# A GNN layer on one core: the last edge chunk moved with 128 partitions, chunk 0's messages earlier, two powers joined

## The reference, cut to what matters

```python
h = jnp.maximum(_layernorm(x), 0.0)
xn = layernorm(h, g1, b1)
msg = relu(xn[src] + edge_attr)
aggr = segment_sum(msg, dst, num_segments=N)
t = (1.0 + eps_gin) * xn + aggr
t = relu(t @ Wg1 + bg1) @ Wg2 + bg2
y = h + t
f = gelu(layernorm(y, g2, b2) @ Wf1 + bf1) @ Wf2 + bf2
out = x + y + f
```

## Time and profile before

| | |
|---|---|
| runs | 1043.13, 1045.61, 1047.68 us |
| median | 1045.61 us |
| profiled execution, its own time | 1042.96 us |
| its span (first to last instruction) | 1041.2 us |
| mean granted TensorE clock | 0.985 of full speed |
| PE busy | 982.8 us, 94% |
| DVE busy | 965.1 us, 93% |
| ACT busy | 852.8 us, 82% |
| POOL busy | 825.9 us, 79% |

### The profile page before, as it was taken

One profiled execution on the slowest core, in us unless ns is written; L12 is line 12 of the kernel. 1 busy time (PEld: TensorE's weight loads), 2 busy tenths in 40 slices (PEclk: granted clock), 3 DMA queues, 4 the chain that ended last, 5 costly groups with the idle time before them and its releaser, 6 DMA issues. The chain is left out here.

```text
span 1041.2 us, 23085 instructions
## 1 busy us (share of the span) xinstructions
PE 982.8 (94%) x6684; PEld 857.0 (82%) x6684; DVE 965.1 (93%) x3499; ACT 852.8 (82%) x2158; POOL 825.9 (79%) x510
## 2 busy tenths in 40 slices
PE   1569999999999999999999999999999999999978
PEld 0357888988889889889888889889889889888867
DVE  5979999999999999999999999999999999998642
ACT  1458888898888988988888988988988988978853
POOL 7788888888788888888888888888888888876610
PEclk9869999999999999999999999999999999999999
DMA  7856766877886654555654664654654554543221
GB/s 259 228 165 162 204 172 179 242 230 220 253 238 157 160 130 118 157 133 117 156 135 116 154 139 116 157 136 115 158 134 116 150 140 117 125 105 81 51 60 41
DMA packets 110468, 156.87 MB, mean 151 GB/s; under 512 B 24835, under 2 KB 50607, under 8 KB 110334
## 3 DMA queue, kind: packets, MB, share of 16 engines
q1 hardware_dynamic: 70358, 128.99, 39.0%
q0 software_dynamic: 37760, 25.66, 17.7%
q10 hardware_dynamic: 2216, 0.66, 0.3%
HBM read 90.61 MB, written 64.61 MB: 149 GB/s over the span
## 5 line engine op out<-in xcount | busy, mean ns | idle before, releaser
L451 POOL DMA_INDIRECT aggr_sums<-e_merged,e_index x196 | 339.2, 1731 | 80.6 <-issue 70.7
L939 PE MATMUL p_out<-wf,n_act 128*128 128x128 f32 x3136 | 370.5, 276 | 1.6
L939 PEld LDWEIGHTS p_out<-wf,n_act 128*128 128x128 f32 x3136 | 357.7, 191 | 6.9 <-DVE p_out L855 5.9
L460 POOL TENSOR_TENSOR n_rstd<-n_var,minus_half 128x16 f32<-128x16 f32 (+3 forms) x102 | 259.7, 2557 | 48.3 <-DVE n_var L835 32.2
L532 ACT ACTIVATE n_act<-p_f,bf1e_col 128x512 f32<-128x512 f32 x392 | 256.2, 680 | 35.2 <-PE p_f L902 31.3
L440 POOL DMA_INDIRECT e_x<-in_x,e_cols x196 | 223.2, 1139 | 61.0 <-issue 59.4
L902 PE MATMUL p_f<-n_z2T_high,wf_low 128*128 128x512 f32 x392 | 202.0, 515 | 5.6 <-DVE n_z2T_low L701 4.8
L902 PE MATMUL p_f<-n_z2T_high,wf_high 128*128 128x512 f32 x392 | 155.1, 396 | 0.0
L902 PE MATMUL p_f<-n_z2T_low,wf_high 128*128 128x512 f32 x392 | 154.6, 394 | 0.0
L687 DVE BATCH_NORM_STATS2 n_stat<-n_x 128x6 f32<-128x256 f32 x392 | 140.3, 418 | 0.6 <-issue 0.4
L614 ACT ACTIVATE n_inT<-p_in 128x512 f32<-128x512 f32 x98 | 58.5, 597 | 99.0 <-PE p_in L946 99.0
(11 more groups left out here) (85 smaller groups left out, 1455.4 us busy)
## 6 DMA issues: line engine op xcount, KB each, us to landing
n_x<-in_x SPq DMA_DIRECT2D x97, 256.0 KB, 3.0
n_aggr<-aggr_sums SPq DMA_DIRECT2D x97, 256.0 KB, 2.7
out_dram<-n_out SPq DMA_DIRECT2D x97, 256.0 KB
aggr_sums<-zeros SPq DMA_DIRECT2D x26, 512.0 KB, 5.2
e_dst<-in_dst_rows SPq DMA_DIRECT2D x49, 256.0 KB, 3.8
e_attr<-in_attr SPq DMA_DIRECT2D x48, 256.0 KB, 3.5
aggr_sums<-zeros SPq DMA_DIRECT2D x12, 1024.0 KB, 5.7
e_x<-in_x,e_cols POOLq DMA_INDIRECT x196, 3.7
```

Of the source, the lines that this page charges most:

```text
L451: nc.gpsimd.indirect_dma_start(out=aggr, out_offset=bass.IndirectOffsetOnAxis(ap=e_index[0:r, s, j:j + 1], axis=0), in_=e_merged[0:r, s, j ...
L460: return nc.gpsimd.tensor_tensor(n_rstd[0:r, s, lo:hi], n_var[0:r, s, lo:hi], minus_half[0:r, 0:(hi - lo) * J].rearrange("p (a j) -> p a j ...
L939: last = nc.tensor.matmul(p_out[0:b.rows, j, :], n_act[:, k, j, 0:b.rows], wf2[:, k, :], start=False, stop=(k == KF - 1), skip_group_check ...
```

## The change

`gather` and `scatter_pair` take all 128 partitions in every chunk, also in chunk 48. For the scatter the index rows 96 to 127 of chunk 48 are first filled with `spare`; then rows 0 to 105 are written as before. The gather of chunk 48 reads on partitions 106 to 127 whatever indices chunk 45 left in the same buffer, and the scatter adds what chunk 45 left in `e_merged` there to spare rows; nobody reads either. `FIRST_JOINED` becomes 2: the powers of chunks 2 and 3 join those of blocks 0 and 2 in column 2, which is empty that early. The message of chunk 0 is issued by ACT ahead of the relu of chunk 1.

```diff
+        s_spare_rows = sem("s_spare_rows")
-        FIRST_JOINED = 4
+        FIRST_JOINED = LEAD - 1
+        def joined_column(c):
+            return 3 if block_beside(c) >= 3 else 2
             def gather(c, columns):
-                r, s = c.rows, c.slot(3)
+                s = c.slot(3)
 ...
-                        out=e_x[0:r, s, j, :], out_offset=None, in_=x,
-                        in_offset=bass.IndirectOffsetOnAxis(ap=e_cols[0:r, s, 0, j:j + 1], axis=0),
+                        out=e_x[0:P, s, j, :], out_offset=None, in_=x,
+                        in_offset=bass.IndirectOffsetOnAxis(ap=e_cols[0:P, s, 0, j:j + 1], axis=0),
             def scatter_pair(c, g):
 ...
-                            ap=e_index[0:r, s, j:j + 1], axis=0),
-                        in_=e_merged[0:r, s, j, :], in_offset=None,
+                            ap=e_index[0:P, s, j:j + 1], axis=0),
+                        in_=e_merged[0:P, s, j, :], in_offset=None,
 ...
-                        assert together and block_beside(c) == b.k
+                        assert together == (joined_column(c) == 3) and block_beside(c) == b.k
                         pool.wait_ge(s_evar, c.at + 1)
-                    power(b.rows, b.slot(8), 0, 4 if with_chunk else 3 if together else 2).then_inc(s_nrstd, 1)
+                    power(b.rows, b.slot(8), 0, 2 + together + with_chunk).then_inc(s_nrstd, 1)
 ...
+            def messages(c):
+                if c is not None:
+                    act.wait_ge(s_esum, c.at + 1)
+                    reached(act, s_emm, c.at - 2)
+                    nc.scalar.activation(e_msg[0:c.rows, c.slot(3)], e_sum[0:c.rows, c.slot(3)],
+                                         ACT.Relu).then_inc(s_emsg, 1)
 ...
-                if 0 in halves and (c := edge(3)) is not None:
-                    act.wait_ge(s_esum, c.at + 1)
-                    reached(act, s_emm, c.at - 2)
-                    nc.scalar.activation(e_msg[0:c.rows, c.slot(3)], e_sum[0:c.rows, c.slot(3)],
-                                         ACT.Relu).then_inc(s_emsg, 1)
+                if 0 in halves and not alone(node, apart):
+                    messages(edge(3))
+                elif 1 in halves and alone(node, apart):
+                    messages(edge(2))
 ...
-                    to = n_var[0:r, block_beside(c) % 8, 3] if joined(c, apart) else e_var[0:r, s, 1]
+                    to = n_var[0:r, block_beside(c) % 8, joined_column(c)] if joined(c, apart) else e_var[0:r, s, 1]
 ...
+                    if r < P:
+                        lo = r // 32 * 32
+                        nc.vector.tensor_copy(e_index[lo:P, s], spare[lo:P]).then_inc(s_spare_rows, 1)
+                        dve.wait_ge(s_spare_rows, 1)
                     dve.wait_ge(s_eextra, c.at + 1)
 ...
-                        rstd = n_rstd[0:r, block_beside(ending) % 8, 3]
+                        rstd = n_rstd[0:r, block_beside(ending) % 8, joined_column(ending)]
```

## The result

The changed kernel takes 1036.36 us (median of 5, 1035.8 to 1038.11), the kernel before 1047.13 us in the same comparison (1043.13 to 1047.77). The ratio is 0.9906, with an interval of 0.9887 to 0.9925: 9.8 us less (7.9 to 11.8). The forecast was 9.6 us less and 1036.0 us. The profiled execution has a span of 1034.6 us against 1041.2 (1031.6 was forecast for it); the one of before was among the fastest of its kernel, so the two spans lie only 6.6 us apart.

The account below looks back on a forecast made before the run. PE and DVE are over 99% busy in the middle, POOL close behind; start, chunk 48's gather and end are left. 6.9 + 1.5 + 0 + 1.2 = 9.6 us off 1045.6 gives 1036.0 us, range 1032.3 to 1040.0.

Parts of the forecast that it names:

- The end: Before block 96: chunk 48's scatters on 128 partitions land sooner, removing PE's 5.23 us wait and its slow clock; 6.9 us.
- PE's gap: Before block 96's transposes: PE's 5.23 us without work goes completely, with 3.3 us to spare.
- The bound without the clock: Lower bound at block 96: 5.2 us gained if PE's clock falls anyway.
- the 1.7 us of the clock: After PE's wait before block 96: clock stays at 2.4 instead of 1.2 GHz for 3.60 us, gaining 1.7 us.
- The share of 0.13: Mean DMA share while chunk 48's 106-partition scatters run alone, read as 2 of 16 engines.
- The gathers: Chunk 48's gathers on 128 partitions: `n_aggr` load lands in 2.8 instead of 4.8 us, PE's wait goes; 1.5 us.
- The spare rows: One DVE copy and a wait for chunk 48 only, 0.1 to 0.3 us, hidden by DVE's lead over PE; taken as 0.
- The start: Chunk 0's earlier message and the joined powers: gathers of chunks 4 and 5 earlier, DVE waits less; 1.2 us.
- The rule on the shared port: Skill's rule that GpSimd SBUF reads shut out two-input DVE operations; the start would bring 0.2 us; not taken.
- That start and gathers bring nothing: Rival: only the 6.9 us before block 96 is gained, so 1038.7 us; chance 15%.
- A slow scatter from chunk 48's rows: Rival: chunk 48's scatter stays slow on 128 partitions because of its rows, so 1042.9 us; chance 4%.
- POOL's phase: Rival: POOL falls into a worse phase from 90 to 900 us, losing 12.3 us, so 1048.3 us; chance 4%.

Follow-up runs that it names:

- the four narrow ones: Traces of the four kernels with chunk 48's scatters on 106 partitions; from block 87 to 97 they take 91.20 us in the mean.
- the one with 107: Changed kernel with chunk 48's scatters on 107 partitions instead of 128; span of its one execution 1052.8 us.
- the four narrow traces: Traces of the four kernels with chunk 48's gathers on 106 partitions; blocks 83 to 87 take 40.4 us in the mean, 38.2 with wide gathers.
- the start alone: Changed kernel with chunk 48's gathers and scatters back on 106 partitions; ratio 0.9979 to the kernel before, 2.2 us less.
- the gathers alone: Kernel before with only chunk 48's gathers put on 128 partitions; ratio 0.9967, 3.5 us less.
- both widths: Kernel before with chunk 48's gathers and scatters on 128 partitions, early powers and message unchanged; ratio 0.9904, 10.1 us less.
- Moving the zeros away: Changed kernel with some or all writes of zeros to the table moved from even to odd steps; ratios 0.9894 (some) and 0.9948 (all).

## Why the prediction was right, point by point

**The end (6.9 us).** Right in mechanism and size. The second pair was to land at 983.6, the load to be there at 986.6 to 987.7, and PE's gap to go with 3.3 us to spare; `n_in` started at 987.22 and was 4.2 us early. The end from block 87 on is 7.0 us shorter than in the trace of before, 7.4 against the mean of the four narrow ones. The bound without the clock (5.2) is excluded, and the 1.7 us of the clock are seen by themselves (42.0 against 43.7 us from the transposes on).

One piece of the evidence was read wrongly. The share of 0.13 in the earlier trace rows was taken for 2 of 16 engines. The first 3.2 us of that window hold no packet at all; while the packets of the two scatters run, the share is twice as high, and with 107 partitions it is nearly the same. The windows are those of the kernel before and of the one with 107:
```profile
974.00:981.00 7.00, 7.00 (x47) 5.92 (x46) 5.72 (x20) 6.18 (x15) 5.18 (x2) 1.00 0.26 21
```
```profile
977.00:987.50 10.50, 10.50 (x69) 8.96 (x68) 7.93 (x23) 9.12 (x24) 6.13 (x2) 1.00 0.25 14
```
So the share does not tell the number of engines, and that 0.13 came out as 2 of 16 was luck. The conclusion holds by the widths and the packet counts above.

**The gathers (1.5 us, from 0 to 2.2).** Right in its place, too small in size: the traces give 2.2 us, the times 3.5 (1.7 to 5.1). What I took from the earlier trace rows was the wait of one execution, and it was the mildest of four: PE lost 1.7 us there, and 2.2 to 2.7 in the others. I had also only priced the load of `n_aggr` that lands late beside the gather, and that was the case in only two of the four narrow traces (4.8 and 5.4 us to landing). In the other two this load landed in 2.7 and 2.8 us, as it does elsewhere, and DVE waited later, for the gathered rows of chunk 48 (3.1 and 3.4 us). With the start alone, in DVE's timeline:
```profile
931.66 0.76 DVE L699 BATCH_NORM_STATS2 e_stat<-e_x 106x6 f32<-106x256 f32 x2 [3.11 <-DMA e_x<-in_x,e_cols]
```
That the load shares engines with the gather, as the prediction put it, was not tested by itself; what is shown is that the wait comes with the narrow gathers (four of four) and mostly goes with them (eight of ten). The wait of 1.78 us that was left in the first trace after was another case: its load was issued at 907.27, 4.4 us after the second scatter (902.91), where before it was 3.6, and DVE could start only 3.9 us after that issue. Why is open.

**The spare rows (0).** The copy takes DVE 0.17 to 0.40 us in the ten traces that have it. Nothing of it shows in the stretch, but a cost of some tenths could not: with both edits on chunk 48 it is as short as with the gathers alone within 1 us, the one odd trace aside.

**The start (1.2 us, from 0 to 2.25).** The steps up to POOL were right: the first scatter at 25.74 instead of 28.46, the last gather of chunk 4 at 50.56 instead of 51.88. The step that failed is "DVE waits 3.56 us for its last column, so DVE gains 0.9": it takes the landing time as fixed. At that time the DMA engines are busy with loads and zeros (share 0.72 from 50 to 57 us before, 0.75 after), and a gather that is issued earlier waits longer: 51.88 to 57.08 is 5.2 us before, 50.56 to 56.53 is 6.0 after; in the mean of the four traces with the old start and the seven with the new one it is 5.6 and 6.0. Moving the zeros away cut this time by 1.7 us, so they set a good part of the landing. What reaches DVE is 0.6 to 0.7 us in the mean of all traces. How much of it reaches the end is not settled: the times give 2.2 us (0.7 to 3.7) alone, and none beside both widths, with some 3 us of uncertainty, and the middle varies by more than that from trace to trace.

**The rule on the shared port** of the Trainium skill, page "SBUF — State Buffer", section "SBUF: two separate sides" (by it a widened power would hold DVE 0.5 us more), is not borne out here: in the kernel before, `n_zg` with its two SBUF inputs takes 1.13 us for its four parts at 887.75, in the middle of a power that runs from 887.67 to 889.98. In that trace 366 of the 392 parts lie wholly inside a power of POOL, and they take 342 ns in the mean, as the others do (347).

**The sum.** By the traces, 7.4 + 2.2 + 0 and whatever of 0 to 1 us is left of the start make 9.6 to 10.6, against 9.8 (7.9 to 11.8) and 10.3 (8.1 to 12.4) measured. That the total lies so near the forecast is in part luck: the end and the gathers gave more than forecast, the start less. By the times, the parts don't add up as well: 8.7 + 3.5 + 2.2 = 14.4 us, more than the whole. Each has an uncertainty of some 1.6 us, and all three are set against the same runs of the kernel before, so that an error in these counts three times; that this is the reason is not shown.

**The rivals.** That start and gathers bring nothing is excluded for the gathers (3.5 us, 1.7 to 5.1), not for the start. A slow scatter from chunk 48's rows is excluded by the widths. Of POOL's phase, which was to cost up to 12 us in the middle, the traces show nothing beyond the 0.9 us between the two means above, which is less than the traces of one start differ among themselves.

## What to carry to other kernels

Look at the tail tile's partition count as a number with divisors: an indirect DMA on 106 or 124 partitions is slower than one on 112, 120 or 128, and padding it with rows that go nowhere is cheaper than sending fewer. A wait that the trace puts to an engine that had no part in it can be a DMA, as the one at 911.22 was; query when that landed. A DMA share averaged over a window that begins before the first packet says little; count the packets instead. And when an issue moves earlier, ask whether the landing moves too: beside DMA engines that were busy to 0.7 it moved by some 0.6 of 1.0 us here.

## What the runs showed of the hardware that was not expected

POOL's own time for a scatter goes with the same divisor: 1.5 to 1.6 us where it is 15 or 16, 2.3 for 4, 2.8 for 2, 4.2 for 1. None of the expectations for 107 and 124 had priced it. It grows with the packets (128 of them for one scatter on 112 partitions, 1728 on 107), by some 1.7 ns for each, an estimate from these two. Beside narrow gathers something else can be late: a 256 KB load issued by SP took 4.8 and 5.4 us in two of four traces, where 2.8 is usual; in the nine traces with wide gathers that have its landing it took 2.8 to 3.2.
